# Scatter of the expert lists with four indirect transfers under way, on four semaphores

## The chip, the core and the metric

The kernel runs on one core of one Trainium2 chip. The metric is device time in microseconds (us); three runs of the kernel before took 1248.61, 1250.51 and 1252.53 us, median 1250.51.

## The reference, cut to what matters

Two blocks, each an attention over a short context and a feed-forward part, are applied to 4096 tokens of width 512. The change touches the last part, a mixture of experts with 8 routed experts and one shared one:

```python
dyn_logits = full_logits[:, :E_DYN]                      # 4096 tokens x 8 experts
mult, sel = _sparse_mixer(dyn_logits)                    # up to 4 experts for each token
mask_dyn = (rw > 0).astype(jnp.int32)
cap = max(int(np.ceil(T / E_DYN * CAPACITY_FACTOR)), MIN_CAPACITY)          # 640
mask_dyn = mask_dyn * (jnp.cumsum(mask_dyn, axis=0) <= cap)
...
y_dyn = jnp.einsum('tei,ehi->teh', jax.nn.silu(g) * u, dyn_down_w)
out = jnp.einsum('te,teh->th', global_w[:, :E_DYN], y_dyn)
y_sh = jnp.einsum('tfi,fhi->tfh', jax.nn.silu(gs) * us, sh_down_w)
out = out + jnp.einsum('tf,tfh->th', global_w[:, E_DYN:], y_sh)
```

Each expert takes at most 640 tokens. The kernel therefore computes a routed expert for the tokens of its own list alone, and needs the eight lists (token number and weight, 640 places each) before the first of them can start.

## The kernel before, in words

The program has four stages. `front` does the first attention and its feed-forward part, `attention1` the second attention, `shared` the shared expert and the routing, `experts` the eight routed experts. Tokens are handled in 32 tiles of 128, or in 8 groups of 512. Each engine has its instructions in one fixed order; engines wait for one another by semaphores that only count up. There is no scheduler at run time.

**Routing.** In the stage `shared`, VectorE works out for each token its up to four experts, the place in each expert's list and the weight. The result is the tiles `index` and `load`, 128 tokens x 32 tiles x 4 choices. Its last instruction is on L1770, and it raises the semaphore `lists`.

**Scatter.** GpSimd then issues 128 indirect transfers (L1629), one for each tile and choice. Each writes 128 records of 8 bytes from SBUF to the tensor `lists` in HBM, at the places that `index` names; records out of bounds are dropped. A transfer raises its semaphore by 16 when it has landed. Transfer n uses semaphore n mod 2 and is issued only when transfer n-2 has landed (L1628), so at most two are under way.

**After the scatter**, on the same queue: both semaphores must be full (L1633), the finished lists are loaded into SBUF (L1888), and ten gathers fetch the rows of experts 0 and 1 from `xn_rows`, five of 128 rows for each (L1791).

**TensorE meanwhile.** It works on the shared expert, unit after unit (64 units of 128 hidden columns for 512 tokens). From unit 24 on a unit is seven products of half size each (L2132, 42 matmuls of 256 columns) and the product with the down weights of an earlier unit, 12 matmuls of 512 columns (L2125). After the last unit's products its order is: transposes of the first 128 gathered rows of expert 0 (L2456), `down` of unit 62 (L2125), transposes of the next 128 rows, `down` of unit 63, and then expert 0's first product (L121). The first transposes wait for all five gathers of expert 0. Between the two transposes ScalarE and VectorE write the rows' high and low halves (L2329, L2399) and unit 63's hidden values (L1903, L1963).

**Semaphores.** Semaphores of the stage `front` are used again in later stages, through a small class that adds the value already reached (`Again`, and `need`). A list `done.again` names those that are free.

Of the kernel before, what the change touches and what calls it, by code (L numbers as in the profile page):

```python
# [25 lines left out]
ALU = mybir.AluOpType  # L26
ACT = mybir.ActivationFunctionType
# [6 lines left out]
NT = T // P  # L34
# [163 lines left out]
def front(g, io, m, banks):  # L198
# [861 lines left out]
    done.engines = sync, gpsimd, scalar, vector, tensor  # L1060
    done.again = [(x, 1) for x in (r_s2, r_bc, r_b, b_hi, b_lo, b_prod, col_mm, dot_ok, id16_ok)]
    done.again += [(x, 2) for x in (r_s1, memsets, col_ok, row_sum, row_nb, b_mm, b_ok, ctx_hi, ctx_lo, rounds)]
# [20 lines left out]
def attention1(g, io, m, banks, f):  # L1083
# [32 lines left out]
    w_in, w_scaled, w_hi, w_lo = (m.sem(n) for n in ("w_in", "w_scaled", "w_hi", "w_lo"))  # L1116
    gw_in, gw_hi, gw_lo = m.sem("gw_in"), m.sem("gw_hi"), m.sem("gw_lo")
    xs_in = m.sem("xs_in")
# [96 lines left out]
    def vector(dve):  # L1215
# [90 lines left out]
        def step(t):  # L1306
            maximum(t - 1, 3)
            prob_low(t - 1, 0)
            query_low(t + 1)
            rows_low(t + 2)  # L1310
            yield
            prob_low(t - 1, 1)
            maximum(t, 0)
            weighted(t - 2)
            logits(t - 5)
            maximum(t, 1)
            prob_low(t - 1, 2)
            residual(t - 3)
            gate_stats(t - 3)
            maximum(t, 2)  # L1320
            aggregate(ln, t + 5)
            stats(ln, t + 6)
            first_rows(t + 3)
            prob_low(t - 1, 3)
            output_low(t - 2)
            aggregate(lg, t - 3)
            gate_low(t - 4)
            inverse_sums(t - 1)
            if t == 2:
                dve.wait_ge(gw_hi, 1)  # L1330
                dve.scalar_tensor_tensor(gws[:, :, 1], gwf[:, :, :], WS, gws[:, :, 0], ALU.mult,
                                         ALU.subtract).then_inc(gw_lo, 1)
        return step, None

    def scalar(act):
# [46 lines left out]
        def step(t):  # L1382
# [18 lines left out]
            if t == 1:  # L1401
                act.wait_ge(gw_in, 16)
                act.activation(gws[:, :, 0], gwf[:, :, :], ACT.Copy, scale=WS).then_inc(gw_hi, 1)
        return step, None

    def tensor(pe):
# [108 lines left out]
        def gate_logits(u):  # L1515
            if live(u):
# [3 lines left out]
                need(pe, s["l_ok"], u)  # L1520
                pe.wait_ge(gw_lo, 1)
                for k in range(KC):
# [46 lines left out]
class Route:  # L1569
# [3 lines left out]
    def __init__(self, sem, g):  # L1573
# [49 lines left out]
        def scatter(pool, io):  # L1623

            need(pool, lists, 1)
            for n in range(NT * TOPK):
                t, k = divmod(n, TOPK)
                need(pool, listed[n % 2], 16 * (n // 2))  # L1628
                pool.indirect_dma_start(  # L1629
                    out=io["lists"], out_offset=bass.IndirectOffsetOnAxis(ap=index[:, t, k:k + 1], axis=0),  # L1630
                    in_=load[:, t, k, :], in_offset=None, bounds_check=E * CAP - 1, oob_is_err=False) \
                    .then_inc(listed[n % 2].handle, 16)
            for turn in listed:  # L1633
                need(pool, turn, 16 * NT * TOPK // 2)

# [872 lines left out]
def stages(nc, g, io):  # L2508


    with ExitStack() as ctx:
# [4 lines left out]
        def sem():  # L2516
            return Again(*free.pop())
        g.x_out = sem()
        second = attention1(g, io, Scope(nc, ctx, "attention1"), banks, first)
        spare = Scope(nc, ctx, "moe")  # L2520
        chain = spare.sem("lists_and_added")
        turns = [spare.sem(f"turn{n}") for n in range(2)]
        g.soft = Again(chain, 0), [Again(turn, 0) for turn in turns], Again(chain, 16)
        g.ex_x_in = [Again(turn, 16 * NT * TOPK // 2) for turn in turns]
        g.ex_added = Again(chain, 16 + 16)
# [177 lines left out]
```

## Time and profile before

| | |
|---|---|
| Median of three runs | 1250.51 us (1248.61 to 1252.53) |
| Profiled execution, its own time | 1257.6 us, the span from first to last instruction; no other time of it is recorded |
| TensorE | 1189.3 us busy, 95% of the span |
| VectorE, ScalarE, GpSimd | 76%, 56%, 47% |
| Scatter, from its first issue to its last landing | 781.3 to 1061.3 us |
| First work of the routed experts on TensorE | 1076.6 us |
| Granted TensorE clock, mean | 0.990 |

An instruction's row in a trace gives its start and its length. For an indirect transfer issued by GpSimd the length is that of the issue alone; when it landed shows in what waited for it. The idle time in square brackets is that of the engine before the instruction, with what ended it. Idle time matters only on an engine for which the others wait.

### The profile page before, as it was taken

How to read it: one execution, taken by the hardware profiler on the slowest of the kernel's cores; microseconds unless marked ns; L12 is line 12 of the kernel's file. 1: busy time of each engine (PE TensorE's matmuls, PEld its weight loads, DVE VectorE, ACT ScalarE, POOL GpSimd, SP SyncE). 2: the span in 40 equal slices, each digit the busy share in tenths (PEclk: the TensorE clock that was granted, in tenths of full speed). 3: DMA queues.
4: the chain of work that ended last, by engine and by line, in shares of the span. 5: the costliest groups of instructions: out<-in, count | busy, mean ns of one | idle time of the engine just before them, and what ended most of it. 6: DMA issues, size and time to landing. Idle time of an engine off the chain costs nothing.

```text
span 1257.6 us, 29419 instructions
## 1 busy us (share of the span) xinstructions
PE 1189.3 (95%) x10692; PEld 822.8 (65%) x10692; DVE 950.4 (76%) x2006; ACT 708.7 (56%) x1988; POOL 589.7 (47%) x685
## 2 busy tenths in 40 slices
PE   6888998799999999999999999999999998799996
PEld 3555665588888888786444445777777776466663
DVE  5889898899999999896677777777777775445460
ACT  4377788799899999896344322222222231365552
POOL 0047668737666667733200000445544345466744
PEclk9999999999999999999999999999999999899999
DMA  9522033134445454643870141221314320799987
GB/s 346 210 60 76 1 32 46 43 111 142 165 135 169 159 172 148 181 157 119 153 196 1 41 127 34 68 44 60 69 34 108 96 68 2 220 254 242 256 139 96
DMA packets 157567, 150.28 MB, mean 119 GB/s; under 512 B 78544, under 2 KB 111472, under 8 KB 157424
## 3 DMA queue, kind: packets, MB, share of 16 engines
q1 hardware_dynamic: 139584, 125.94, 35.5%
q0 software_dynamic: 13248, 21.15, 8.9%
q10 hardware_dynamic: 4592, 1.32, 0.6%
q8 instruction: 86, 1.41, 0.5%
q14 instruction: 57, 0.47, 0.1%
HBM read 84.93 MB, written 57.19 MB: 113 GB/s over the span
## 4 chain that ended last, share of the span: by engine, by line
PE 59%; DMA 17%; issue 8%; DVE 8%; POOL 5%; ACT 3%; ACTq 0%; SPq 0%; POOLq 0%; DVEq 0%
PE bank L121 28%; DMA lists<-att_land 14%; PE bank L1503 6%; PE bank L2125 5%; PE bank L955 4%; POOL lists L1629 4%; PE bank L1435 4%; PE bank L1456 3%; PE bank L1450 2%; PE bank L1421 2%; DMA q_rows<-att_land 1%; PE bank L1024 1%; ACT att_land L1353 1%; PE bank L872 1%; PE bank L891 1%
## 5 line engine op out<-in xcount | busy, mean ns | idle before, releaser
L1629 POOL DMA_INDIRECT lists<-att_land x128 | 134.4, 1050 | 310.7 <-DVE att_land L1770 166.8
L1353 ACT ACTIVATE att_land<-bank,att_land 128x120 f32<-128x120 f32 x512 | 178.3, 375 | 11.3 <-DVE att_land L1221 11.2
L2125 PE MATMUL bank<-att_land 128*128 128x512 f16 x768 | 177.3, 381 | 0.6 <-DVE program_logits L1304 0.6
L1952 ACT ACTIVATE att_land<-program_x 128x512 f32<-128x512 f32 x40 | 25.2, 631 | 195.2 <-DVE program_x L2094 165.1
L2125 PEld LDWEIGHTS bank<-att_land 128*128 128x128 f16 x768 | 75.4, 98 | 82.9 <-issue 2.0
L121 PE MATMUL bank<-program_xs,program_wgu 128*128 128x512 f16 x576 | 128.7, 379 | 0.6 <-DVE att_land L1729 0.6
L1353 ACT ACTIVATION_READ_ACCUMULATOR att_land<-bank,att_land 128x1 f32 x512 | 112.8, 221 | 0.0
L121 PE MATMUL bank<-att_land 128*128 128x128 f16 (+1 forms) x1560 | 101.0, 221 | 0.5 <-DVE att_land L1278 0.5
L121 PEld LDWEIGHTS bank<-program_xs,program_wgu 128*128 128x128 f16 x576 | 56.2, 98 | 67.5 <-DVE att_land L1729 1.1
L1221 DVE TENSOR_REDUCE att_land<-bank 128x4 f32<-128x480 f32 x128 | 82.4, 644 | 20.5 <-PE bank L1421 20.1
L1503 PE MATMUL bank<-att_land 128*128 128x512 f16 x384 | 93.4, 379 | 0.0
L121 PEld LDWEIGHTS bank<-att_land 128*128 128x128 f16 x1560 | 91.1, 98 | 3.6 <-DVE att_land L1278 0.7
L1227 DVE TENSOR_TENSOR att_land<-bank,att_land 120x512 f16<-120x512 f32 x128 | 86.9, 679 | 3.5 <-ACT att_land L1343 3.1
L1343 ACT ACTIVATE att_land<-bank 120x512 f16<-120x512 f32 x128 | 77.8, 610 | 19.0 <-PE bank L1435 15.7
L2132 PE MATMUL bank<-program_x 128*128 128x256 f16 x720 | 85.1, 273 | 0.0
L2294 POOL DMA_INDIRECT out_rows<-program_x,att_land x40 | 64.7, 1617 | 35.5 <-ACT program_x L2335 25.4
L121 PE MATMUL bank<-program_x 128*128 128x256 f16 (+2 forms) x504 | 80.5, 318 | 0.6 <-DVE program_x L2387 0.6
L1903 ACT ACTIVATE att_land<-att_land 128x512 f16<-128x512 f32 x64 | 40.2, 629 | 71.1 <-PE bank L2125 30.6
L1435 PE MATMUL bank<-program_ident,att_land 128*120 128x128 f32 x512 | 78.0, 275 | 1.4 <-DVE att_land L1227 1.4
L2132 PEld LDWEIGHTS bank<-program_x 128*128 128x128 f16 x720 | 70.4, 98 | 8.2
L428 POOL TENSOR_TENSOR program_x<-program_x,att_land 128x512 f32<-128x512 f32 x32 | 40.9, 1277 | 69.8 <-ACT att_land L546 69.8
L1435 PEld LDWEIGHTS bank<-program_ident,att_land 128*120 128x120 f32 x512 | 59.3, 138 | 13.7 <-issue 2.0
(305 smaller groups left out, 2817.2 us busy)
## 6 DMA issues: line engine op xcount, KB each, us to landing
att_land<-q_rows SPq DMA_DIRECT2D x96, 128.0 KB, 2.6
xn_rows<-att_land SPq DMA_DIRECT2D x37, 256.0 KB, 3.7
out_rows<-att_land SPq DMA_DIRECT2D x37, 256.0 KB, 6.4
q_rows<-att_land SPq DMA_DIRECT2D x32, 256.0 KB, 2.9
xt_tiles<-att_land SPq DMA_DIRECT2D x32, 256.0 KB, 2.1
x_rows<-program_x SPq DMA_DIRECT2D x8, 1024.0 KB, 4.8
att_land<-x_rows SPq DMA_DIRECT2D x8, 1024.0 KB, 5.6
program_xs<-xt_tiles SPq DMA_DIRECT2D x28, 256.0 KB
```

The lines of the kernel that those rows point to most:

```text
L121: last = pe.matmul(out, lhs(a, k), rhs(b, k), start=n == 0, stop=n == len(terms) - 1)
L955: last = pe.matmul(out, lhs, rhs, start=k == 0 and i == 0, stop=k == KC - 1 and i == 2)
L1221: dve.tensor_reduce(nmax[:, u % 2, c], ps_s[c % 2][:, :, :], AX.X, ALU.max, negate=True).then_inc(c4["max"], 1)
L1227: dve.tensor_tensor(pT[0:J, c, 1], ps_p[c % 2][0:J], pT[0:J, c, 0], ALU.subtract).then_inc(c4["p_lo"], 1)
L1343: act.activation(pT[0:J, c, 0], ps_p[c % 2][0:J], ACT.Copy).then_inc(c4["p_hi"], 1)
L1353: last = act.activation(prob[:, c, h, :], ps_s[c % 2][:, h, :], ACT.Exp, bias=nmax[:, u % 2, c, h:h + 1], accum_out=rsum[:, u % 2, n:n + 1])
L1435: last = pe.transpose(ps_p[c % 2][0:J, h, :], prob[:, c, h, :], g.ident[:, :])
L1503: last = pe.matmul(ps_y[:, :], oT[:, u % 2, a, k, :], g.wo1[:, b, k, :], start=k == 0 and n == 0, stop=k == KC - 1 and n == 2)
L1629: pool.indirect_dma_start(out=io["lists"], out_offset=bass.IndirectOffsetOnAxis(ap=index[:, t, k:k + 1], axis=0), in_=load[:, t, k, :], in ...
L2125: last = pe.matmul(ps_y[i][:, :], hid[:, c % 2, a, i * P:(i + 1) * P], wd[:, q, c, :], start=c == 0 and n == 0, stop=c == NC - 1 and n == 2)
L2132: last = pe.matmul(out, lhs(a, k), rhs(q, k), start=n == 0, stop=n == len(terms) - 1)
L2294: pool.indirect_dma_start(out=io["out"], out_offset=bass.IndirectOffsetOnAxis(ap=lst[:, u * CT + n, 0:1], axis=0), in_=res[:, c, n, :], in ...
```

## The change: four semaphores in turn

Transfer n of the scatter now uses semaphore n mod 4 and is issued when transfer n-4 has landed. Two semaphores more are needed; two that belonged to the gating weights (`gw_hi`, `gw_lo`) are replaced by used ones of the stage `front`, and the list of these is two longer. The gathers keep two of the four.

```diff
@@ front
-    done.again = [(x, 1) for x in (r_s2, r_bc, r_b, b_hi, b_lo, b_prod, col_mm, dot_ok, id16_ok)]
+    done.again = [(a["stats"], NT), (q["stats"], NT)]
+    done.again += [(x, 1) for x in (r_s2, r_bc, r_b, b_hi, b_lo, b_prod, col_mm, dot_ok, id16_ok)]
@@ attention1
-    gw_in, gw_hi, gw_lo = m.sem("gw_in"), m.sem("gw_hi"), m.sem("gw_lo")
+    gw_in, gw_hi, gw_lo = m.sem("gw_in"), g.gw_hi, g.gw_lo
@@ Route.scatter
             for n in range(NT * TOPK):
                 t, k = divmod(n, TOPK)
-                need(pool, listed[n % 2], 16 * (n // 2))
+                need(pool, listed[n % 4], 16 * (n // 4))
                 pool.indirect_dma_start(
                     out=io["lists"], out_offset=bass.IndirectOffsetOnAxis(ap=index[:, t, k:k + 1], axis=0),
                     in_=load[:, t, k, :], in_offset=None, bounds_check=E * CAP - 1, oob_is_err=False) \
-                    .then_inc(listed[n % 2].handle, 16)
+                    .then_inc(listed[n % 4].handle, 16)
             for turn in listed:
-                need(pool, turn, 16 * NT * TOPK // 2)
+                need(pool, turn, 16 * NT * TOPK // 4)
@@ stages
-        g.x_out = sem()
+        g.x_out, g.gw_hi, g.gw_lo = sem(), sem(), sem()
-        turns = [spare.sem(f"turn{n}") for n in range(2)]
+        turns = [spare.sem(f"turn{n}") for n in range(4)]
-        g.ex_x_in = [Again(turn, 16 * NT * TOPK // 2) for turn in turns]
+        g.ex_x_in = [Again(turn, 16 * NT * TOPK // 4) for turn in turns[0:2]]
```

No instruction that computes or moves data changes its place on any engine. On GpSimd, at the start of the scatter, the program of before stands so (`moe_turn0` and `moe_turn1` are the two semaphores):

```order
482:480 L1629 DMA lists<-att_land 5120x2
483:481 L1629 DMA lists<-att_land 5120x2 [waits moe_turn0]
484:482 L1629 DMA lists<-att_land 5120x2 [waits moe_turn1]
485:483 L1629 DMA lists<-att_land 5120x2 [waits moe_turn0]
486:484 L1629 DMA lists<-att_land 5120x2 [waits moe_turn1]
```

The same place in the changed program, where the line is L1630:

```order
482:480 L1630 DMA lists<-att_land 5120x2 x3
483:481 L1630 DMA lists<-att_land 5120x2 [waits moe_turn0]
484:482 L1630 DMA lists<-att_land 5120x2 [waits moe_turn1]
485:483 L1630 DMA lists<-att_land 5120x2 [waits moe_turn2]
486:484 L1630 DMA lists<-att_land 5120x2 [waits moe_turn3]
```

Three transfers in place of one follow the first without a wait, and each later wait is for the transfer four earlier.

## Rows read from the trace of the kernel before

**Rows 1.** Chain that ended last, by line: shares of the span

```profile
PE bank L121 28%; DMA lists<-att_land 14%; PE bank L1503 6%; PE bank L2125 5%; PE bank L955 4%; POOL lists L1629 4%; PE bank L1435 4%; PE bank L1456 3%; PE bank L1450 2%; PE bank L1421 2%; DMA q_rows<-att_land 1%; PE bank L1024 1%; ACT att_land L1353 1%; PE bank L872 1%; PE bank L891 1%
```

**Rows 2.** Waits: engine and line waited for, us in total, times, longest

```profile
PE bank L2456 <- DMA att_land<-xn_rows,att_land: 12.5, 1, 12.5
POOL lists L1629 <- DMA lists<-att_land: 107.7, 50, 8.5
POOL lists L1629 <- issue: 36.2, 77, 6.6
```

**Rows 3.** Stretches: busy us of each engine, granted clock, DMA share, GB/s

```profile
1000.00:1050.00 50.00, 50.00 (x378) 36.65 (x376) 34.66 (x71) 14.49 (x25) 26.25 (x24) 1.00 0.18 43
1060.00:1070.00 10.00, 4.10 (x28) 2.54 (x26) 2.88 (x7) 0.63 (x1) 3.66 (x3) 0.81 0.20 9
1070.00:1080.00 10.00, 3.37 (x11) 1.81 (x12) 1.29 (x2) 1.11 (x2) 7.56 (x9) 0.51 0.71 206
```

**Rows 4.** Timeline of PE around the turn to the experts: start, us

```profile
1063.28 0.82 PE L2132 MATMUL bank<-program_xs,program_x 128*128 128x256 f16 x6
1076.63 1.12 PE L2456 MATMUL bank<-program_ident,att_land 128*128 128x128 f32 x4 [12.53 <-DMA att_land<-xn_rows,att_land]
1077.54 3.86 PE L2125 MATMUL bank<-att_land 128*128 128x512 f16 x12
1081.24 0.60 PE L2456 MATMUL bank<-program_ident,att_land 128*128 128x128 f32 x4
1081.67 2.75 PE L2125 MATMUL bank<-att_land 128*128 128x512 f16 x12
1084.27 2.78 PE L121 MATMUL bank<-program_x,att_land 128*128 128x256 f16 x24
```

**Rows 5.** Timeline of POOL, end of the scatter, and expert 2's first gather

```profile
1058.15 1.47 POOL L1629 DMA_INDIRECT lists<-att_land  x1 [0.31 <-issue]
1061.28 2.01 POOL L1888 DMA_DIRECT2D att_land<-lists  x1 [1.66 <-DMA lists<-att_land]
...
1094.29 0.94 POOL L1791 DMA_INDIRECT att_land<-xn_rows,att_land  x1 [13.77 <-DMA out_rows<-att_land]
```

**Rows 6.** Timeline of POOL: first scatter, first and last of eleven long waits

```profile
781.28 1.10 POOL L1629 DMA_INDIRECT lists<-att_land  x1 [166.78 <-DVE att_land L1770]
...
806.52 1.43 POOL L1629 DMA_INDIRECT lists<-att_land  x1 [3.60 <-DMA lists<-att_land]
...
1053.94 0.97 POOL L1629 DMA_INDIRECT lists<-att_land  x1 [2.80 <-DMA lists<-att_land]
```

**Rows 7.** Groups of POOL from 781 to 1062 us: count, busy us, mean ns, idle

```profile
L1629 POOL DMA_INDIRECT lists<-att_land x128 | 134.4, 1050 | 310.7 <-DVE att_land L1770 166.8 <-DMA lists<-att_land 107.7 <-issue 36.2
```

**Rows 8.** Timeline of POOL, first and last of eleven issues in a row

```profile
1035.43 0.97 POOL L1629 DMA_INDIRECT lists<-att_land  x1 [6.65 <-issue]
...
1050.17 0.97 POOL L1629 DMA_INDIRECT lists<-att_land  x1 [0.32 <-issue]
```

**Rows 9.** Timeline of ACT and DVE, what prepares the last `down` product

```profile
1065.26 0.69 DVE L2100 SCALAR_TENSOR_TENSOR att_land<-program_x,att_land 128x512 f32<-128x512 f32 x1 [0.69 <-ACT att_land L1952]
...
1078.28 0.62 ACT L1903 ACTIVATE att_land<-att_land 128x512 f16<-128x512 f32 x1
...
1079.03 0.68 DVE L1963 TENSOR_TENSOR att_land<-att_land 128x512 f16<-128x512 f32 x1
```

**Rows 10.** Waits of PE from 1085 to 1250 us, all there are

```profile
PE bank L2456 <- DVE program_xs L2395: 0.9, 1, 0.9
PE bank L121 <- DVE program_x L2387: 0.6, 1, 0.6
```

**Rows 11.** Timeline of PE, three `down` products one unit apart

```profile
1030.68 2.75 PE L2125 MATMUL bank<-att_land 128*128 128x512 f16 x12
1037.86 2.75 PE L2125 MATMUL bank<-att_land 128*128 128x512 f16 x12
1045.03 2.75 PE L2125 MATMUL bank<-att_land 128*128 128x512 f16 x12
```

More of the change, by code:

```diff
@@ L1329, in step @@
             if t == 2:
-                dve.wait_ge(gw_hi, 1)
+                need(dve, gw_hi, 1)
                 dve.scalar_tensor_tensor(gws[:, :, 1], gwf[:, :, :], WS, gws[:, :, 0], ALU.mult,
-                                         ALU.subtract).then_inc(gw_lo, 1)
+                                         ALU.subtract).then_inc(gw_lo.handle, 1)
         return step, None
@@ L1402, in step @@
                 act.wait_ge(gw_in, 16)
-                act.activation(gws[:, :, 0], gwf[:, :, :], ACT.Copy, scale=WS).then_inc(gw_hi, 1)
+                act.activation(gws[:, :, 0], gwf[:, :, :], ACT.Copy, scale=WS).then_inc(gw_hi.handle, 1)
         return step, None
@@ L1520, in gate_logits @@
                 need(pe, s["l_ok"], u)
-                pe.wait_ge(gw_lo, 1)
+                need(pe, gw_lo, 1)
                 for k in range(KC):
```

## The prediction

> **What bounds the kernel now.** I read the chain of waits first. It is mostly TensorE's, but the scatter of the lists, as transfers and as issues, has 18% of the span in it [rows 1]. A share of the chain is not yet a loss, so I asked the table of waits what TensorE itself lost there. It is one wait: before the first transposes of expert 0 it stood idle for 12.5 us, until that expert's gathers had landed [rows 2]. The table of stretches shows the rest: from 1000 to 1050 us TensorE is busy throughout, from 1060 to 1080 us for 7.5 of 20 us, and the granted clock falls from 1.00 to 0.51, its level of 1.2 GHz [rows 3]. Last I read the timeline. The shared expert's last product ends at 1063.28 + 0.82 = 1064.10, the transposes start at 1076.63, and expert 0's first product at 1084.27 [rows 4].
>
> What TensorE waited for is one queue, GpSimd's. The last scatter's issue ends at 1058.15 + 1.47 = 1059.62; behind it stand the landing, the load of the lists from 1061.28 on and the gathers [rows 5], and then the transposes at 1076.63. This tail behind the last issue is 17.0 us long. To cost TensorE nothing, the issues would have to end at 1064.10 - 17.0 = 1047.1, that is 12.5 us earlier. They take 278.3 us, from 781.28 [rows 6] to 1059.62; 4.5% of it is needed.
>
> **The change, part by part.**
>
> *The scatter.* It keeps its 128 issues, 134.4 us busy [rows 7]. Between them stand 50 waits for a transfer that had not landed, 107.7 us, and 77 gaps that no transfer is shown to cause, 36.2 us [rows 2]. One of these is 6.65 us [rows 8]; the other 76 have a mean of (36.2 - 6.65) / 76 = 0.39 us. With four under way a wait is for a transfer issued two places further back. So it shrinks by about two issues with their gaps, 2 x (0.97 + 0.39) = 2.7 us, and a wait shorter than that goes. Eleven waits are longer, the first 3.60 us and the last 2.80 us [rows 6], the longest 8.5 [rows 2]; what the eleven have above 2.7 us sums to 11.1 us. The new length is 134.4 + 127 x 0.39 + 6.3 (the odd gap above the mean) + 11.1 = 201 us, and the scatter ends at about 982 us. Bounds: with no wait for a transfer left it is 184 us (ending at 965), with none shortened the 278 us of before. Whether it saves 94 us, 77 us (my value) or only 12.5 us, the wait of TensorE is gone.
>
> *The tail.* Load and gathers then lie at about 984 to 1000 us, beside the shared expert, in a stretch in which the DMA engines are busy for about 0.18, and are gone from the one from 1070 us on, where this share is 0.71 [rows 3]. TensorE has no idle time between 1000 and 1050 us that a transfer could lengthen, so I price this at nothing; the nearest bound is 1 us for one late load.
>
> *What TensorE gains.* From the end of the last product to expert 0's first it now takes 1084.27 - 1064.10 = 20.17 us. Without the wait, and with the clock still at its upper level of 2.4 GHz, the steps go at the pace of the second pair in [rows 4]: transposes 1081.67 - 1081.24 = 0.43, `down` 1084.27 - 1081.67 = 2.60, each twice, 6.06 us. The gain is 14.1 us: 12.5 of idle time and 1.6 from the first pair, which ran at the lower clock (3.86 us for the same 12 matmuls that take 2.75).
>
> *What is late next.* The second `down` could start at 1064.10 + 0.43 + 2.60 + 0.43 = 1067.6. It needs L1963, behind L1903 and L2100: 1065.26 + 0.69 + 0.62 + 0.68 = 1067.3 [rows 9]. That is 0.3 us before it is needed; if a hand-over slips, it costs a few tenths. Expert 0's later steps, the three transposing DMAs and the next weights among them, are issued behind these and move with them. GpSimd's next wait, for the shared expert's output rows before expert 2's gathers [rows 5], is for a transfer that also moves. From 1085 us on TensorE has 1.5 us of waits in all [rows 10], so an earlier start is an earlier end.
>
> *The semaphores.* The two that are used again were last raised in `front`; the waits on them compare with a constant, and no engine has an instruction more in its path. Priced at nothing. The two further waits at the scatter's end are GpSimd's and lie in idle time; a gap of 0.3 us [rows 5] bounds each.
>
> *Sum.* On the profiled execution's own time: 1257.6 - 14.1 = 1243.5. That execution is 7.1 us (0.6%) longer than the median of the runs. If the excess is spread over everything, the stall in the timed runs is the same, and they go to 1250.5 - 14.1 = 1236.4. If all of it lay in the scatter, the one long piece that waits for transfers, their stall is 12.5 - 7.1 = 5.4 us and the gain 5.4 + 1.6 = 7.0: 1243.5. I stand near the first, because the scatter is only 278 of 1258 us, and predict 1237.5.
>
> **The Trainium skill against the rows.** In the eleven issues without a wait for a transfer, from 1035.43 to 1050.17, they follow each other every 1.47 us [rows 8], so nine of them must have landed at that pace. The Trainium skill, "DMA: Bandwidth & Descriptors", section "Queues, rings and completion order", says that a semaphore's increment lands only after every earlier write of that DMA engine, across its queues. By that rule depth buys nothing in a wait that another queue's slow write causes. If the eleven long waits stayed whole for that reason, each would have 2.7 us more, 30 us in all, and the scatter would end at about 1012 us, still before 1047. No row here shows which writes were waited for.
>
> **Rivals.**
>
> *The queue serves one by one, at the present mean.* The 278.3 us are 2.17 us for each transfer. If that is the server's pace, depth only makes the queue longer, and the time stays 1250.5. For it: 50 of 127 issues wait. Against it: [rows 8], and that the other 77 issues found a transfer landed less than 2 us after its neighbour.
>
> *The stall was smaller in the timed runs, or another wait takes its place.* 1243.5 at the worst of the first; with 3 to 8 us of new waiting for the hidden values or the transposing DMAs 1240 to 1245. For it: the 7.1 us above, and the 3.9 us between the lowest and the highest run, which fits a kernel whose end hangs on transfers. Against it: the margins in [rows 9, 10].
>
> *GpSimd's denser issues slow VectorE, and TensorE waits for it: slower.* While the scatter runs, each of 39 units needs VectorE's sums on time. The price is 39 x the delay of one unit: from 14.1 / 39 = 0.36 us a unit on the kernel is slower than before, at 0.6 us it is 1250.5 - 14.1 + 23.4 = 1260. Against it: where the eleven issues stand, GpSimd already works at the rate that I expect, 1.47 us an issue, and that unit takes 1045.03 - 1037.86 = 7.17 us, the unit before it, for most of which GpSimd stood still, 7.18 [rows 8, 11]. The Trainium skill, "SBUF — State Buffer", section "Who interferes with whom", has the rule behind this rival, an exclusive lock on the ports that the two engines share; the trace shows no price of it for TensorE at this rate.
>
> **How the numbers follow.** Stall gone whole, 1235 to 1240: 0.76. Smaller stall or a new wait, 1240 to 1246: 0.14. One by one, unchanged: 0.06. Slower: 0.04. Under 3.8 us (0.3%) a difference can't be told from none here. The first two cases lie beyond that, but for a small part of the second: faster 0.89, same 0.07, slower 0.04. The range takes in the first two cases and 3.4 us below 1236.4, since runs of one kernel differ by as much: 1233 to 1245.
>
> **What would show it.** Right: the last scatter issue ends between 965 and 1010 us and few of its gaps are waits for a transfer; TensorE's wait at the first transposes is under 0.5 us, and the clock stays at 1.00 from 1060 to 1080 us; from the last product to expert 0's first it takes 6 to 7 us; units stay at 7.2 us. Wrong: a scatter that still ends after 1047 (one by one), units of 7.5 us or more (VectorE), or a new idle time of TensorE between 1060 and 1090 us.

## The result, and the profile after

The changed kernel takes 1407.13 us (median of 4 runs, 1405.12 to 1410.14), the kernel before in the same comparison 1251.52 us. The ratio is 1.1249, interval 1.1217 to 1.1281: 12.5% slower where 1.1% faster was forecast. In what follows a run's time is some 1.7 us above the span of its trace (1405.12 and 1403.4 for the profiled execution of the changed kernel).

The page of the changed kernel shows the place at a glance. These are its slices of 35.1 us each (busy tenths, the granted clock in tenths of full speed), and the shares of the chain:

```profile
PE   7889997999999999999999740122999999999997
POOL 0166777377677673320000577773000000046654
PEclk9999999999999999999999975555999999999999
DMA  9421051344444555395040300003303141099996
...
PE 71%; another core or an unknown queue 9%; DVE 8%; issue 4%; ACT 2%; DMA 2%; DVEq 1%; POOL 1%; ACTq 0%; SPq 0%; POOLq 0%
```

For five slices, 807 to 982 us, TensorE's row shows hardly any work; in four of them its clock is granted at about 0.5, the level of 1.2 GHz, and in four the DMA engines are nearly idle as well. GpSimd stands at 7 in the first four of the five: it is the scatter. The table of stretches gives the amounts (columns as in [rows 3]):

```profile
800.00:900.00 100.00, 22.57 (x132) 14.14 (x132) 12.59 (x28) 4.12 (x7) 73.98 (x76) 0.61 0.06 10
900.00:1000.00 100.00, 34.62 (x188) 20.32 (x189) 20.89 (x43) 7.18 (x13) 47.49 (x48) 0.61 0.16 36
1000.00:1050.00 50.00, 50.00 (x377) 36.56 (x376) 37.98 (x81) 12.62 (x23) 0.00 (x0) 1.00 0.14 47
```

In experiment 9 below, whose TensorE never waits there, 100 us hold 752 matmuls; from 800 to 900 us the changed kernel's row has 132. Once GpSimd is quiet (0.00 from 1000 us) all is as in [rows 3] again.

The scatter itself did what the change wanted, and more. GpSimd's timeline (start, length, idle time before it), which answers to [rows 6]:

```profile
779.28 1.10 POOL L1630 DMA_INDIRECT lists<-att_land  x1 [166.77 <-DVE att_land L1771]
...
806.01 0.97 POOL L1630 DMA_INDIRECT lists<-att_land  x1 [2.75 <-DMA lists<-att_land]
...
947.03 0.97 POOL L1630 DMA_INDIRECT lists<-att_land  x1 [0.30 <-issue]
949.70 2.01 POOL L1889 DMA_DIRECT2D att_land<-lists  x1 [1.70 <-DMA lists<-att_land]
956.38 1.01 POOL L1792 DMA_INDIRECT att_land<-xn_rows,att_land  x1 [4.67 <-DMA att_land<-lists]
```

The last issue ends at 948.0, after 168.7 us where 201 was forecast. The waits in the table answer to [rows 2]. The long DVE row, 48.9 us, is the largest part of the 9% of the chain, some 122 us, that stand there under "another core or an unknown queue":

```profile
PE bank L2133 <- issue: 114.1, 16, 47.9
...
DVE program_x L2090 <- remote: 48.9, 1, 48.9
...
POOL att_land L1792 <- DMA out_rows<-att_land: 272.1, 1, 272.1
...
POOL lists L1630 <- DMA lists<-att_land: 4.6, 5, 2.8
```

Of 50 waits for a transfer, 107.7 us, five are left, 4.6 us. GpSimd then stands for 272.1 us with its work done. TensorE pays for it. Where its own timeline shows the first lateness, about 9 us after the scatter's start, and what it looks like in the middle:

```profile
788.05 0.82 PE L2133 MATMUL bank<-program_xs,program_x 128*128 128x256 f16 x6
788.99 0.83 PE L2133 MATMUL bank<-program_xs,program_wgu 128*128 128x256 f16 x6
...
799.92 0.83 PE L2133 MATMUL bank<-program_x,program_wgu 128*128 128x256 f16 x6 [3.12 <-issue]
...
890.23 1.46 PE L2133 MATMUL bank<-program_xs,program_wgu 128*128 128x256 f16 x6 [47.90 <-issue]
...
907.03 1.46 PE L2133 MATMUL bank<-program_x 128*128 128x256 f16 x6 [14.06 <-issue]
923.83 1.46 PE L2133 MATMUL bank<-program_x 128*128 128x256 f16 x6 [15.34 <-issue]
```

Six matmuls that took 0.65 us from start to next start ([rows 4]: 0.82 long) now come every 16.8 us. VectorE, which adds up their results, is no cause: its instructions keep their 0.42 us, and it is idle before each of these, "remote" being a release that the profile can't name:

```profile
840.05 0.42 DVE L2077 TENSOR_TENSOR program_x<-bank,program_x 128x256 f32<-128x256 f32 x1 [10.91 <-remote]
...
889.75 0.42 DVE L2090 TENSOR_TENSOR program_x<-bank,program_x 128x256 f32<-128x256 f32 x1 [48.94 <-remote]
906.55 0.42 DVE L2092 TENSOR_TENSOR program_x<-bank,program_x 128x256 f32<-128x256 f32 x1 [16.38 <-remote]
923.35 0.42 DVE L2095 TENSOR_TENSOR program_x<-bank,program_x 128x256 f32<-128x256 f32 x1 [16.38 <-remote]
```

Each of these waits for one product more. 6 matmuls of 256 columns take 16.80 us, and the 18 between 840.05 and 889.75 us (12 of 512 columns, 6 of 256) take 49.70 us: 2.80 and 2.76 us for each matmul, whatever its width. So what is slow isn't the multiplying, but something that happens once for each instruction.

What do VectorE's rows wait for? By the program, L2090, L2092 and L2095 need the fifth, sixth and seventh product of their unit. TensorE's rows start these long before (the last matmuls of the fifth, then the sixth, then the seventh):

```profile
821.05 0.38 PE L2133 MATMUL bank<-program_xs,program_wgu 128*128 128x256 f16 x2 [0.43 <-issue]
828.61 1.46 PE L2133 MATMUL bank<-program_x,program_wgu 128*128 128x256 f16 x6 [7.17 <-issue]
840.87 1.46 PE L2133 MATMUL bank<-program_xs,program_x 128*128 128x256 f16 x6 [10.80 <-issue]
```

At 779 to 782 us VectorE gets such a product 0.04 us after its last matmul ends in TensorE's row. Here it gets the three 68, 76 and 81 us after. At 842 us the rows have thus started some 30 matmuls whose results have not reached VectorE. A start in TensorE's row is here no sign that the work is being done, and the idle time beside it ("issue") is no sign that there is none: the product that TensorE starts next, at 890.23, may by the program start only when L2090 has ended, at 890.17, and L2090 waits for the fifth. From 930 to 953 us TensorE's own rows show the pace one by one, first with 512 columns, then with 256:

```profile
933.14 0.59 PE L2126 MATMUL bank<-att_land 128*128 128x512 f16 x1 [2.42 <-issue]
935.94 0.59 PE L2126 MATMUL bank<-att_land 128*128 128x512 f16 x1 [2.21 <-issue]
...
949.94 0.37 PE L2133 MATMUL bank<-program_xs,program_wgu 128*128 128x256 f16 x1 [2.43 <-issue]
952.74 0.37 PE L2133 MATMUL bank<-program_xs,program_wgu 128*128 128x256 f16 x1 [2.42 <-issue]
```

The last two stand behind the scatter's last issue (948.0). The pace does not end with it: VectorE gets the next two products at 956.25 and the third at 972.35, which is 32.9 us for 12 matmuls and 16.1 us for 6. From 948.0 to 956.38 GpSimd issues no indirect transfer, then the ten gathers, to 968.65. Only behind these is TensorE free again.

After the last product everything goes as forecast; the three rows answer to [rows 4]:

```profile
1224.03 0.82 PE L2133 MATMUL bank<-program_xs,program_x 128*128 128x256 f16 x6
1224.68 0.60 PE L2457 MATMUL bank<-program_ident,att_land 128*128 128x128 f32 x4
...
1230.74 2.78 PE L121 MATMUL bank<-program_x,att_land 128*128 128x256 f16 x24
```

No wait at the transposes, and 6.06 us from them to expert 0's first product. The account of the two traces, from starts of matmuls:

| | before | after | difference |
|---|---|---|---|
| first half-size product of unit 24 on | 776.3 | 774.4 | -1.9 |
| from there to the last one's last matmul | 287.5 | 450.2 | +162.7 |
| from there to expert 0's first product | 20.4 | 6.2 | -14.3 |
| from there to the end | 173.4 | 172.6 | -0.7 |
| span | 1257.6 | 1403.4 | +145.8 |

### The profile page after: what moved, and what is told of

Its sections match the earlier page's. It is cut to its first block, busy times and chain, and to the rows that moved or that the text cites. A ratio compares the mean times of both kernels' runs of the same rounds, so it can differ in the third digit from the quotient of the medians.

```text
span 1403.4 us, 29420 instructions
## 1 busy us (share of the span) xinstructions
PE 1202.2 (86%) x10692; PEld 825.5 (59%) x10692; DVE 950.4 (68%) x2006; ACT 709.1 (51%) x1988; POOL 580.5 (41%) x685
## 3 DMA queue, kind: packets, MB, share of 16 engines
q10 hardware_dynamic: 4592, 1.32, 0.5%
## 4 chain that ended last, share of the span: by engine, by line
PE 71%; another core or an unknown queue 9%; DVE 8%; issue 4%; ACT 2%; DMA 2%; DVEq 1%; POOL 1%; ACTq 0%; SPq 0%; POOLq 0%
PE bank L121 25%; PE bank L2133 12%; PE bank L2126 11%; PE bank L1504 5%; PE bank L955 3%; PE bank L1436 3%; PE bank L1457 2%; PE bank L1451 2%; PE bank L1422 2%; PE bank L1024 1%; DVEq L63 1%; DMA q_rows<-att_land 1%; ACT att_land L1354 1%; PE bank L872 1%
## 5 line engine op out<-in xcount | busy, mean ns | idle before, releaser
L1630 POOL DMA_INDIRECT lists<-att_land x128 | 125.8, 983 | 209.7 <-DVE att_land L1771 166.8
L1792 POOL DMA_INDIRECT att_land<-xn_rows,att_land x40 | 42.0, 1051 | 304.9 <-DMA out_rows<-att_land 272.1
L2133 PE MATMUL bank<-program_xs,program_wgu 128*128 128x256 f16 x480 | 69.4, 279 | 65.8 <-issue 63.4
L2133 PE MATMUL bank<-program_x 128*128 128x256 f16 x720 | 89.5, 280 | 29.6 <-issue 29.6
L2133 PEld LDWEIGHTS bank<-program_xs,program_wgu 128*128 128x128 f16 x480 | 46.6, 99 | 85.3 <-issue 66.5
L121 PEld LDWEIGHTS bank<-program_xs,program_wgu 128*128 128x128 f16 x576 | 56.3, 98 | 67.5 <-DVE att_land L1730 1.1
```

Source lines behind the costliest of these rows:

```text
L121: last = pe.matmul(out, lhs(a, k), rhs(b, k), start=n == 0, stop=n == len(terms) - 1)
L1630: pool.indirect_dma_start(out=io["lists"], out_offset=bass.IndirectOffsetOnAxis(ap=index[:, t, k:k + 1], axis=0), in_=load[:, t, k, :], in ...
L2133: last = pe.matmul(out, lhs(a, k), rhs(q, k), start=n == 0, stop=n == len(terms) - 1)
```

## The experiments

The theory formed on the trace above: GpSimd's indirect issues with no more than 0.3 us between them, kept up for more than some 8 to 10 us, hold TensorE up. It was first put as a pace: the expectations call it the pace theory. The rivals: the semaphores that are used again; the number of transfers under way; the flood of 8-byte records; the transfers of any kind that GpSimd issues. Every kernel is the changed one with the edit shown. "Products" is the second row of the account, 287.5 us where nothing disturbs it.

**1. The four semaphores, but two under way.**

```diff
-                need(pool, listed[n % 4], 16 * (n // 4))
+                if n >= 2:
+                    need(pool, listed[(n - 2) % 4], 16 * ((n - 2) // 4 + 1))
```

> The changed kernel with its four semaphores and its new allotment of used ones, but transfer n waits for transfer n-2, as before. Pace theory (TensorE is starved where GpSimd issues indirect transfers without a pause, every 1.275 us): 1250 us, as before. Number theory (three or four transfers under way starve it, at any pace): 1250 us too. Semaphore theory (the other semaphores or their number do it): 1400 us or more.

Measured 1251.29 us, ratio 1.0003 (0.9969 to 1.0037), products 291.5. The semaphores and their reuse cost nothing.

**2. Three under way.**

```diff
-                need(pool, listed[n % 4], 16 * (n // 4))
+                if n >= 3:
+                    need(pool, listed[(n - 3) % 4], 16 * ((n - 3) // 4 + 1))
```

> Three transfers under way, n waits for n-3, everything else as in the changed kernel. Pace theory: a transfer lands 3 to 5 us after its issue, so GpSimd still pauses often; scatter about 220 to 230 us long, TensorE mostly unhurt, 1237 to 1260 us. Number theory: units of over 8 us while the scatter runs, 1300 us or more.

Measured 1408.01 us, ratio 1.1268 (1.117 to 1.1367), products 445.5. Three is as bad as four. The forecast that GpSimd would still pause often was wrong: 49 issues in a row stand less than 0.4 us apart, so both theories allow the result. The loss does not grow with the number; it comes whole once the waits are gone.

**3. Four under way, but every eighth issue waits until all have landed.**

```diff
                 need(pool, listed[n % 4], 16 * (n // 4))
+                if n % 8 == 0 and n > 0:
+                    for m in (n - 3, n - 2, n - 1):
+                        need(pool, listed[m % 4], 16 * (m // 4 + 1))
```

> Four under way, but at every eighth transfer GpSimd waits until all have landed, a pause of about 3 us after some 10 us. Pace theory: the pause frees TensorE as the one of 2.75 us at 803 us did; scatter about 211 us long, 1237 to 1245 us. Number theory: four under way for three quarters of the time, over 1350 us.

Measured 1300.36 us, ratio 1.0407 (1.0318 to 1.0495), products 339.9. Here rows of eight issues stand apart, and TensorE's gaps stand at their ends. First GpSimd's first pause, then TensorE's first gap:

```profile
792.03 0.97 POOL L1633 DMA_INDIRECT lists<-att_land  x1 [0.30 <-issue]
794.99 0.97 POOL L1633 DMA_INDIRECT lists<-att_land  x1 [1.99 <-DMA lists<-att_land]
```

```profile
791.56 0.82 PE L2136 MATMUL bank<-program_xs,program_x 128*128 128x256 f16 x6
796.25 0.83 PE L2136 MATMUL bank<-program_xs,program_wgu 128*128 128x256 f16 x6 [3.87 <-DVE program_x L2093]
```

The row of eight began at 782.80, and its last issue ends at 793.00. TensorE's own rows have no gap for its first 9.6 us, then they have one, and TensorE works again 3.3 us after the row's end, and 1.8 us after the end of the next row (805.18 and 806.99). VectorE notices earlier: it gets the product whose last matmul ends at 787.82 only at 790.10, 7.3 us after the row's start. The 1237 to 1245 us that were expected assumed that a row of eight is short enough; it isn't.

**4. Four under way, with an instruction between issues that is waited for.** GpSimd clears a small dead tile, and waits for that, before each issue.

```diff
                 need(pool, listed[n % 4], 16 * (n // 4))
+                pool.memset(blank[:, :, 1:2], 0).then_inc(consts.handle, 1)
+                need(pool, consts, 7 + n)
```

> Four under way, with a short memset on GpSimd and a wait for it between two issues, so that one issue follows the other every 1.5 us or more. Pace theory: TensorE keeps its 7.2 us units, scatter about 195 to 210 us, 1237 us. Number theory: with 3 to 5 us from issue to landing two to three are still under way, 1300 us or more.

Measured 1252.65 us, ratio 1.0009 (0.9987 to 1.0031), products 294.1. Issues start every 2.0 us on average and never closer than 1.89 us; until the last of them TensorE has no gap. So four under way are harmless if issued slowly. The time is 15 us above the 1237 that were expected, and not below that of the kernel before. One gap is left, beside the ten gathers, which this kernel issues as before. GpSimd, then TensorE:

```profile
1049.12 1.01 POOL L1794 DMA_INDIRECT att_land<-xn_rows,att_land  x1 [4.72 <-DMA att_land<-lists]
...
1061.00 0.94 POOL L1794 DMA_INDIRECT att_land<-xn_rows,att_land  x1 [0.30 <-issue]
```

```profile
1060.04 0.83 PE L2135 MATMUL bank<-program_xs,program_x 128*128 128x256 f16 x6 [0.58 <-issue]
1064.10 1.46 PE L2135 MATMUL bank<-program_xs,program_wgu 128*128 128x256 f16 x6 [3.23 <-DVE program_x L2092]
```

Again it comes some ten microseconds after the row's start. The gathers read from HBM, with records of other sizes: it isn't what the scatter writes.

**5. The same number of instructions, not waited for.** Between issues GpSimd clears one word; only the clearing before it is waited for, which is done long since.

```diff
                 need(pool, listed[n % 4], 16 * (n // 4))
+                need(pool, consts, 6 + n)
+                pool.memset(g.eps[:, :], EPS).then_inc(consts.handle, 1)
```

> Four under way; a memset of one column stands between two issues, but the issue does not wait for it, so issues should follow each other every 1.4 to 1.6 us (1.275 us in the changed kernel, 1.9 to 2.0 us with the waited-for memset). If what starves TensorE is a pace over some rate between 1.28 and 1.9 us, this tells on which side 1.5 us lies: under the limit 1245 to 1255 us, over it 1270 to 1400 us.

Measured 1398.60 us, ratio 1.1174 (1.1138 to 1.1211), products 446.4. With as many instructions as in experiment 4, and the same waits for transfers in the program, the loss is back. What differs is the time from the end of an issue to the next one, 0.30 us here and 0.93 us there:

```profile
902.23 0.12 POOL L1631 MEMSET program_eps<- 128x1 f32 x1
902.54 0.97 POOL L1632 DMA_INDIRECT lists<-att_land  x1 [0.19 <-issue]
```

```profile
901.29 0.16 POOL L1630 MEMSET att_land<- 128x40 int32 x1
902.22 0.97 POOL L1632 DMA_INDIRECT lists<-att_land  x1 [0.77 <-issue]
```

**6. An eighth of the records.** Each indirect transfer takes 16 partitions; the lists then lack seven eighths of the tokens.

```diff
-                    out=io["lists"], out_offset=bass.IndirectOffsetOnAxis(ap=index[:, t, k:k + 1], axis=0),
-                    in_=load[:, t, k, :], in_offset=None, bounds_check=E * CAP - 1, oob_is_err=False) \
+                    out=io["lists"], out_offset=bass.IndirectOffsetOnAxis(ap=index[0:16, t, k:k + 1], axis=0),
+                    in_=load[0:16, t, k, :], in_offset=None, bounds_check=E * CAP - 1, oob_is_err=False) \
```

> Each of the 128 scatters writes the records of 16 partitions in place of 128 (the lists lack seven eighths of the tokens), four under way, no pause added. Theory issue (it is GpSimd issuing without a pause): TensorE still starved while GpSimd issues every 1.3 us, 1300 us or more. Theory records (it is the flood of 8-byte records in the DMA engines, eight times smaller here): no starvation, about 1240 to 1250 us. If the issues themselves become much shorter, the pace says which rate counts.

Measured 1421.62 us in a single run, products 465.5: no better, rather worse, with the issues a little closer (1.22 us from start to start on average, 1.32 in the changed kernel). An eighth of the records takes nothing off the loss: the flood of records is not the cause. VectorE's rows show the same step for six matmuls, to a hundredth:

```profile
818.93 0.42 DVE L2090 TENSOR_TENSOR program_x<-bank,program_x 128x256 f32<-128x256 f32 x1 [15.39 <-remote]
835.74 0.42 DVE L2092 TENSOR_TENSOR program_x<-bank,program_x 128x256 f32<-128x256 f32 x1 [16.38 <-remote]
852.53 0.42 DVE L2095 TENSOR_TENSOR program_x<-bank,program_x 128x256 f32<-128x256 f32 x1 [16.38 <-remote]
```

**7. Plain transfers of the same tiles, four under way.** They write to another tensor, and the lists stay blank.

```diff
-                pool.indirect_dma_start(
-                    out=io["lists"], out_offset=bass.IndirectOffsetOnAxis(ap=index[:, t, k:k + 1], axis=0),
-                    in_=load[:, t, k, :], in_offset=None, bounds_check=E * CAP - 1, oob_is_err=False) \
+                pool.dma_start(io["lists2"][(n % 40) * P:(n % 40 + 1) * P, :], load[:, t, k, :]) \
```

> The 128 indirect scatters become 128 plain transfers of the same 128 records of 8 bytes from SBUF to another tensor in HBM, still issued by GpSimd with four under way (the lists stay blank). Theory indirect (something in the indirect issue starves TensorE): 1240 to 1250 us. Theory issue or records: starved as before, 1300 us or more, if GpSimd issues them every 1.3 us.

Measured 1249.60 us in a single run, products 293.3, with one gap of 4.1 us, beside its ten gathers. This left open whether the kind of issue or its pauses protected TensorE: no row was longer than four issues of 0.54 us. Experiment 12 settles it.

**8. The waited instruction in the gathers too.** As 4, with the clearing of one word, also once before each gather.

```diff
-            gather_rows(pool, g, io, e)
+            for n in range(CT):
+                pool.memset(g.eps[:, :], EPS).then_inc(routing.consts.handle, 1)
+                need(pool, routing.consts, 7 + NT * TOPK + e * CT + n)
+                pool.indirect_dma_start(
+                    ...
```

> The waited-for memset between all scatters and also between the ten gathers behind them. In the run with paced scatters alone TensorE's products took 294.1 us against 287.5 before, and the units that lagged lay beside the ten gathers issued every 1.25 us. Pace theory: with these paced too the products take 288 us and the kernel about 1245 us, 5 to 7 us under before. If the gathers are not the cause: 1252 us.

Measured 1250.29 us, ratio 0.9978 (0.9959 to 0.9998), products 293.4. The one instruction hardly spread the gathers (0.38 us between them in place of 0.30), and the gap beside them stayed, 3.9 us. As a test of the gathers' pace this kernel is a miss. It has another use: in the scatter it has the same instruction as experiment 5, the clearing of one word, and differs from it in that each issue waits for it. TensorE has no gap in the scatter here. So it is the pause, and not what is cleared, that parts 4 and 5.

**9. Four waited instructions before each gather, one before each scatter.**

```diff
+            for n in range(CT):
+                for pause in range(4):
+                    pool.memset(g.eps[:, :], EPS).then_inc(routing.consts.handle, 1)
+                    need(pool, routing.consts, 7 + NT * TOPK + 4 * (e * CT + n) + pause)
```

> Scatter as in paced (four under way, a waited memset in each gap), and before each of the ten gathers four small waited memsets, so that these too follow each other with pauses. If it is the pace of GpSimd's indirect issues that starves TensorE, the 3 to 4 us gap of TensorE that paced and paced_all showed beside the gathers is gone, no gap over 1 us is left from 780 to 1070 us, the products of the shared expert take 287.5 to 289 us as before, TensorE's wait at the first transposes is under 0.5 us, and the span is 1243 to 1247 us; the median of the timed runs 1245 to 1250, 0.996 to 0.999 of before. If the gap is not from the gathers' pace but from what they read, it stays and the span is 1248 to 1253. A price of the longer tail (about 10 us more on GpSimd, which has 16 us to spare) is not expected.

Measured 1247.62 us (7 runs, 1244.34 to 1250.21), ratio 0.9958 (0.9943 to 0.9973); span 1244.7, products 287.5. Its interval lies below that of no change, by 0.3 to 0.6%. The gathers now start every 1.8 us, all waits of TensorE from 700 us to the end are two in expert 0, and the turn to the experts takes 6.1 us:

```profile
1040.80 1.02 POOL L1899 DMA_INDIRECT att_land<-xn_rows,att_land  x1 [0.28 <-POOL program_eps L1897]
1041.82 0.59 POOL L1897 MEMSET program_eps<- 128x1 f32 x4
```

```profile
PE bank L2466 <- DVE program_xs L2405: 0.9, 1, 0.9
PE bank L121 <- DVE program_x L2397: 0.6, 1, 0.6
```

**10. Rows of four.** As 3, with `n % 4` in place of `n % 8`.

> Every fourth issue waits until all earlier transfers have landed, the three between wait for nothing: bursts of four issues with gaps of 0.3 us (5.1 us from first to last end), then a pause of about 2 us; mean spacing about 1.8 us. If starvation needs a run of unbroken issues longer than 8 to 10 us, the bursts are too short for it: span 1245 to 1256, products of the shared expert under 295 us. If it is the share of short gaps that counts (three of four here, seven of eight in the variant with every eighth, which took 340 us), products take 310 to 325 us and the span is 1270 to 1285.

Measured 1252.42 us, ratio 1.0005 (0.9979 to 1.0032), products 296.1. In the scatter TensorE lost 0.9 us in all, in two gaps; what else is lost lies again beside the gathers (4.8 us of gaps between 1056 and 1064).

**11. The waited instruction before every second issue only.**

```diff
                 need(pool, listed[n % 4], 16 * (n // 4))
+                if n % 2:
+                    pool.memset(blank[:, :, 1:2], 0).then_inc(consts.handle, 1)
+                    need(pool, consts, 7 + n // 2)
```

> The waited memset stands in every second gap only: gaps of about 0.3 and 0.9 us in turn, mean spacing about 1.6 us, no long pause. If only the mean rate counts, with a bound between 1.4 us (starved) and 1.9 us (not), this lies between: products of the shared expert 288 to 350 us, and TensorE's gaps grow slowly through the scatter. If an unbroken run of short gaps is needed, no run here is longer than two issues: products under 296 us and span 1245 to 1256. If any short gap costs, half of what the unpaced version lost: products near 365 us.

Measured 1249.26 us, ratio 0.9978 (0.9946 to 1.0011), products 288.2. Issues at 1.72 us on average, gaps of 0.3 and 0.9 us in turn, and TensorE has no gap beside the scatter. Its ten gathers, at 1012 to 1026 us, cost only 0.3 us, in a row with the same pauses of 0.30 us as the one that cost 4 us in 4: a row of ten is at the edge, and what it costs differs from place to place.

**12. Plain transfers in rows of 64, with no wait.**

```diff
-                need(pool, listed[n % 4], 16 * (n // 4))
-                pool.dma_start(io["lists2"][(n % 40) * P:(n % 40 + 1) * P, :], load[:, t, k, :]) \
+                if n % 64 == 0:
+                    for m in range(4):
+                        need(pool, listed[m], 16 * (n // 4))
+                pool.dma_start(io["lists2"][n * P:(n + 1) * P, :], load[:, t, k, :]) \
```

> All 128 indirect transfers of the scatter are replaced by plain ones of the same source tiles (128 records of 8 bytes each) to another tensor, so the lists hold no tokens; they are issued in two rows of 64 without a wait inside a row, where the earlier variant with plain transfers had four under way and a pause after at most four issues. A row of 64 at 0.54 us an issue is 34 us unbroken, well over the 8 to 10 us after which the unbroken indirect issues starved TensorE. If any unbroken stream of transfers issued by GpSimd starves it, TensorE stands still for most of these 34 us, twice, and the products of the shared expert take 310 to 350 us in place of 287.5. If it is the indirect form, in which GpSimd itself works out the addresses of each record, no gap over 1 us appears from 780 to 900 us and the products take 288 to 295 us, span 1244 to 1252.

Measured 1248.55 us in a single run, products 292.4. GpSimd issued plain transfers for 34.02 us without a pause, and TensorE did not lose a microsecond in these 90 (first the row of GpSimd, then that of the stretches):

```profile
780.14 34.02 POOL L1632 DMA_DIRECT2D lists<-att_land  x64 [166.42 <-DVE att_land L1771]
```

```profile
780.00:870.00 90.00, 90.00 (x681) 66.12 (x680) 65.81 (x142) 21.58 (x40) 67.98 (x128) 1.00 0.44 61
```

The same trace then has ten gathers from 877.35 us on, and there, 9 us later, TensorE's first gap:

```profile
886.39 0.83 PE L2133 MATMUL bank<-program_x 128*128 128x256 f16 x6 [0.77 <-issue]
```

So it is the indirect form.

**All together.** "Longest row" is the most issues of the scatter less than 0.4 us apart, and how long they take.

| kernel | longest row | products, us | span, us |
|---|---|---|---|
| before | 3 (4.2 us) | 287.5 | 1257.6 |
| 9, one wait each, gathers spread | 1 | 287.5 | 1244.7 |
| 11, every second | 2 (3.3 us) | 288.2 | 1247.5 |
| 1, two under way | 2 (3.2 us) | 291.5 | 1246.1 |
| 4, one wait each | 1 | 294.1 | 1253.0 |
| 10, rows of four | 4 (5.9 us) | 296.1 | 1249.9 |
| 3, rows of eight | 8 (11.6 us) | 339.9 | 1297.2 |
| 5, not waited for | 19 (24.2 us) | 446.4 | 1400.5 |
| 2, three under way | 49 (62.4 us) | 445.5 | 1404.3 |
| the change | 64 (81.4 us) | 450.2 | 1403.4 |
| 6, 16 partitions | 67 (78.1 us) | 465.5 | 1419.9 |
| 12, plain transfers | 64 (34.0 us) | 292.4 | 1246.8 |

7 and 8, not in the table, have rows of four plain issues (293.3 us) and of one (293.4). With indirect issues the products are late only in kernels whose rows are eight or longer, but for some microseconds beside the ten gathers (1, 4, 8, 10 and, with their gathers alone indirect, 7 and 12). The mean pace is not what parts them: with an issue every 1.66 us on average experiment 3 loses 52 us, with one every 1.72 us experiment 11 loses 0.7. No kernel has a longest row of five to seven.

## Why the prediction was wrong

**The step that failed.** The sum had a term for the scatter's end and none for what the scatter, so changed, does to the units beside it, but for a rival at 0.04. It measured 162.7 us of the 169.6 between forecast and result. The step behind it is the one that let this pass: that in the stretch of eleven issues "GpSimd already works at the rate that I expect", with units of 7.17 us [rows 8, 11]. Two things were wrong in it. The mean of 1.47 us hid gaps of 0.43 to 0.70 us among those of 0.30, and the longest row of issues closer than 0.4 us in the whole scatter before was three. And the rate to come was taken from the scatter of before, where the wider gaps belong to work that goes on beside it; in the changed kernel the gap was 0.30 us, the mean start to start 1.32. The evidence was of a pace and a length that the change then left. A stretch that is to stand for a future state must match it in the gaps, one by one, and in how long they go on.

**The state keeps itself up.** The forecast took the transfers' latency as given: eleven waits longer than 2.7 us would be left, 11.1 us in all. But when TensorE is held up, so is most of the other traffic (a DMA share of 0.06 from 800 to 900 us, where experiment 1 has 0.24). Transfers land soon, GpSimd finds nothing to wait for, and the row isn't broken. The trace shows the other direction too: the pause of 2.75 us before 806.01 freed TensorE until about 819 us, and the four other waits of the whole scatter sum to 1.9 us. That the shorter latency comes from the missing traffic is an inference; the waits' disappearance, 50 to 5, is shown. Once there, the state can also outlast a pause. In the changed kernel the pace of about 2.7 us a matmul goes on through 8.4 us without an indirect issue, between scatter and gathers, and in experiment 6 through 11.4 us: from 919.88 to 968.23 VectorE waits for 18 matmuls, while the scatter's last issue ends at 935.53 and the gathers begin at 946.97. In experiment 5 TensorE was free 1.2 us after the scatter's last issue, in experiment 2 about 7 us after it. What decides this, no run shows.

**The slower rival** named GpSimd's denser issues and VectorE as the way in which they reach TensorE. The first half was right. The second was not: VectorE's instructions kept their length and it waited itself, and the price was not 0.36 or 0.6 us a unit but up to 2.8 us a matmul. The rule that I had put beside it, the Trainium skill's "SBUF — State Buffer", section "Who interferes with whom", has no such path: it lets only VectorE and GpSimd block each other and says "PE and ACT never wait on anyone". The rows of 907.03 and 923.83 above, and experiments 5 and 8, whose scatters differ in a pause of 0.6 us on GpSimd alone, show that TensorE does wait on something that GpSimd's unbroken row of indirect issues brings about. If the sentence is read so, the measurement decides against it. The section is on the access to SBUF, and whether TensorE is held up there or elsewhere no run shows.

**The rule on completion order**, which would have kept the eleven long waits whole, was not borne out: five waits, 4.6 us, were left. Most other traffic stood still at that time, so this is no clean test of the rule. **One by one** fell as well: the scatter ran at 1.32 us a transfer where 2.17 would have been the server's pace.

**What was right.** TensorE's wait at the transposes was 0.1 us, the steps to expert 0's first product took 6.1 us (6 to 7 forecast), the ten gathers had landed long before they were needed, the two semaphores cost nothing (1.0003), and later stages only moved. In the kernel without the loss, number 9, the sum on the profiled execution comes out: 1243.5 was forecast, its span is 1244.7, of which 1.8 us are a later start of the stage.

**The tail** was priced at nothing, with a bound of 1 us for one late load, for which no row stood. The ten gathers are a row of 0.30 us pauses themselves, 12.3 us long. In the kernels whose scatter does no harm (1, 4, 7, 8 and 12) the products are 4.0 to 6.6 us late, nearly all of it beside the gathers. In the changed kernel TensorE's wait of 19.7 us before 972.83 stands there. In the kernel before, the gathers (1068.0 to 1080.5) stood mostly where TensorE had nothing to do, so their price could not be seen.

**A second term of the sum was mis-sized all the same.** Even that kernel is at 1247.62 us, not 1237.5, and 4.4 us better than the 1252.04 us of before in its comparison. The wait of 12.5 us is that of one execution, whose span of 1257.6 us lies above every other profiled kernel's without the loss. I spread its excess over everything; the measured gain, between 3.4 and 7.1 us by the interval, fits my other reading, in which the timed runs have a stall of about 5 us and gain 7. What the timed runs of before really had in that place no trace shows, so this stays an inference. A gain read from one wait of one execution should have been held against the spread of the runs first.

**What stays open** is which part of the chip TensorE and the indirect issues share. Known is: it costs about 2.8 us for each matmul, whatever its width and whether issues come every 1.32 or 1.22 us; it needs 7 to 10 us of unbroken indirect issues to set in; in experiment 3 it ended at the pauses behind every eighth issue, but after the long rows of the change and of experiment 6 it outlasted 8.4 and 11.4 us without an indirect issue; scatter and gather do it, plain transfers don't, and an eighth of the records does it as well. Larger differences in the amount of data, or other engines in TensorE's place, were not tried.

## What to carry to other kernels

When a change takes waits out of a queue, the pauses go with them: look at what the other engines did while the queue paused, and treat the new, unbroken row as a state that the old trace has never shown. On GpSimd, don't let more than four indirect transfers follow each other at 0.3 us beside TensorE's work (rows of four cost 0.9 us in the whole scatter, rows of eight and the gathers 52, and nothing between was run); a small instruction that is waited for in every second gap (experiment 11) removes the loss at no cost that could be measured. And read a gain from the spread of the runs as well as from the one wait of the profiled one.

## What the hardware showed that was not expected

- TensorE's rows can start matmuls far ahead of their results: in the held-up stretch VectorE gets a product up to 81 us after its last matmul's end in TensorE's row, against 0.04 us otherwise. When a consumer is released by "remote" and the producer's row is idle by "issue", compare the two before calling the producer idle.
- An unbroken row of indirect issues by GpSimd (0.97 us each, 0.30 us apart) slows TensorE from 0.11 us a matmul of 256 columns to 2.8 us, and its granted clock falls to 1.2 GHz with it (0.61 of full speed on average from 800 to 1000 us). 0.6 us more between issues prevents it (1398.60 against 1252.65 us).
- Plain transfers by GpSimd cost 0.54 us each and follow each other without a gap, 64 in 34.02 us, with TensorE at full speed.
- An indirect issue costs GpSimd 0.97 us for 128 records of 8 bytes in the middle of the scatter, and 0.85 us for 16 records (1.22 us from start to start on average): its price is nearly all fixed.
